# A hand-ordered five-engine pipeline: chosen rows sent through memory by index, decays by half the heads, and another order of steps

## The reference

```
x = x + gnn0(layernorm(x), adj)      # MLP, dense attention (512), MLP, masked attention: steps a_*, b_*
x = x + ffn0(layernorm(x))           # 127 chosen rows go through a GELU MLP: steps q_*
x = x + gat1(layernorm(x), adj)      # masked attention: steps g_*
x = x + mamba(layernorm(x))          # conv, silu, decays exp(segsum(dA)), gated norm, product: steps m_*

weights = x @ wr + br                # ffn0, x is layernormed
sel_idx = top_k(weights, 128)[:127]
y = gelu(x[sel_idx] @ w1 + b1) @ w2 + b2
out = zeros.at[sel_idx].set(y * weights[sel_idx]) + x
```

## Time and profile before

| | us |
|---|---|
| median of 3 runs | 3751.22 (3750.86 to 3752.01) |
| the profiled execution, its own time | 3752.41 |
| its span, first to last instruction | 3750.7 |
| PE busy | 3618.9 (96%) |
| PE weight loads busy, beside PE | 3158.1 (84%) |
| DVE busy | 2973.1 (79%) |
| ACT busy | 2364.2 (63%) |
| POOL busy | 993.9 (26%) |

### The profile page before, as it was taken

How to read it: one execution, slowest core, us unless ns; L and a number is a source line. 1 busy time by engine, 2 the same in 40 slices (tenths; PEclk the granted TensorE clock), 3 DMA queues, 4 the chain that set the end, 5 groups by cost and what they waited for, 6 DMA issues and landing times.

```text
span 3750.7 us, 63924 instructions
## 1 busy us (share of the span) xinstructions
PE 3618.9 (96%) x21016; PEld 3158.1 (84%) x21016; DVE 2973.1 (79%) x7729; ACT 2364.2 (63%) x5314; POOL 993.9 (26%) x1821
## 2 busy tenths in 40 slices
PE   6799999999999999999999999999999999999975
PEld 4688888888888888888888888888888888888864
DVE  3468878878888888888888888888887887888875
ACT  2356666667666666666666666666666666666654
POOL 0022232232232232232222223223223223223222
PEclk8899999999999999999999999999999999999998
DMA  3000100100100110110010010010010010010000
GB/s 102 12 26 32 39 28 31 39 28 31 39 28 31 39 36 23 39 39 23 36 39 28 31 39 28 31 39 28 31 39 28 31 39 28 31 39 29 30 29 31
DMA packets 73763, 126.85 MB, mean 34 GB/s; under 512 B 9984, under 2 KB 64128, under 8 KB 65536
## 3 DMA queue, kind: packets, MB, share of 16 engines
q1 hardware_dynamic: 69360, 126.39, 9.8%
q10 hardware_dynamic: 4368, 0.03, 0.1%
HBM read 109.10 MB, written 17.30 MB: 34 GB/s over the span
## 4 chain that ended last, share of the span: by engine, by line
PE 87%; DVE 8%; issue 2%; ACT 1%; POOL 0%; ACTq 0%; DVEq 0%; POOLq 0%
PE A L1199 12%; PE M L1335 7%; PE A L1219 7%; PE Q L1323 6%; PE A L1237 6%; PE A L1188 6%; PE Q L1316 6%; PE M L1369 6%; PE M L1428 6%; PE A L1284 3%; PE A L1246 3%; PE Q L1246 3%; PE Q L1284 3%; PE A L1229 2%; PE M L1357 2%
## 5 line engine op out<-in xcount | busy, mean ns | idle before, releaser
L1199 PE MATMUL A<-w_fc,o1T 128*128 128x256 f32 (+1 forms) x2048 | 454.7, 380 | 3.8 <-ACT o1T L541 3.8
L1199 PEld LDWEIGHTS A<-w_fc,o1T 128*128 128x128 f32 x2048 | 382.9, 189 | 57.8 <-ACT o1T L541 4.0
L433 POOL TENSOR_TENSOR var_m<-mv_m,epsilon 128x2 f32<-128x2 f32 x64 | 12.6, 197 | 1414.7 <-DVE mv_m L813 1414.7
L710 ACT ACTIVATE dec<-cumB,cumcol 128x256 f32<-128x256 f32 (+1 forms) x1024 | 366.2, 443 | 0.0
L1022 DVE SCALAR_TENSOR_TENSOR acc<-M,w_conv,acc 128x255 f32<-128x255 f32 (+2 forms) x768 | 315.0, 470 | 0.0
L1335 PE MATMUL M<-xT_m,w_in 128*128 128x256 f32 x1280 | 297.5, 379 | 0.8 <-DVE tz L1064 0.5
L1219 PE MATMUL A<-h,low 128*128 128x257 f32 (+1 forms) x1024 | 256.4, 395 | 22.9 <-DVE low L854 14.0
L1335 PEld LDWEIGHTS M<-xT_m,w_in 128*128 128x128 f32 x1280 | 237.7, 190 | 32.1 <-DVE tz L1064 2.0
L1323 PE MATMUL Q<-w_down,gsq 128*128 128x256 f32 x1024 | 241.2, 390 | 9.7 <-DVE gsq L995 9.7
L1316 PE MATMUL Q<-selT,w_up 128*128 128x128 f32 x2048 | 249.5, 275 | 0.9 <-ACT selT L646 0.9
L1064 DVE SCALAR_TENSOR_TENSOR tz<-tz,M 128x512 f32<-128x512 f32 x128 | 88.1, 688 | 202.5 <-ACT tz L693 202.5
(11 more groups left out here) (235 smaller groups left out, 8830.3 us busy)
## 6 DMA issues: line engine op xcount, KB each, us to landing
cumB<-cum_dram SPq DMA_DIRECT2D x64, 1024.0 KB, 4.7
x_in<-in_x SPq DMA_DIRECT2D x64, 256.0 KB, 2.8
x<-in_x SPq DMA_DIRECT2D x64, 256.0 KB, 2.9
out<-x3b SPq DMA_DIRECT2D x64, 256.0 KB, 2.8
w_mlp<-in_L_gnn_mlp_w SPq DMA_DIRECT2D x2, 512.0 KB, 6.3
w_fc<-in_L_gnn_W_fc SPq DMA_DIRECT2D x2, 512.0 KB, 8.6
w_up<-in_L_ffn_w SPq DMA_DIRECT2D x1, 1024.0 KB, 11.7
w_down<-in_L_ffn_w SPq DMA_DIRECT2D x1, 1024.0 KB, 12.9
```

The lines of the kernel that those rows point to most:

```text
L710: last = nc.scalar.activation(dec[:, h, :], columns[:, h, :], ACT.Relu, bias=cumcol[:, i, h:h + 1], scale=-1.0)
L1199: last = nc.tensor.matmul(rows1(half, u, 2), o1T[:, k, u * P:(u + 1) * P], w_fc[:, k, half, 0:D + 2 * i], start=(k == 0), stop=(k == KH - 1))
```

## The change

1. `q_gather` no longer forms the chosen rows by four products. DVE `q_rank` also writes `place`, the row number for each row: its rank, or rank + 1 from rank 127 on. A new POOL step `q_send` sends the two tiles of `xn_q` row by row to `sel_dram` with two indexed DMAs. A new SP step `q_sel` waits for both and loads the first 128 rows back to `sel`; PE `q_gather` waits for that and turns `sel` with two transposes. Row 127 is zeroed once, before the first turn.
2. The decays go by halves of the heads: four ACT steps and four DVE mixes instead of two; `m_y.0` waits for the first two mixes, `m_y.1` for all.
3. Long PE steps are two each (`q_ffn2`, `a_mlp2`, `m_z`, `m_out`), DVE's `m_silu` and POOL's `m_dt_log` too.
4. All five lists have another order and partly other lags.
5. DVE's `norm` waits for earlier readers in two cases (`a_xT_ps`, `sel_sent`); `m_scan` waits for the second `dec1` part of the graph before.

```diff
-    "tensor": [('q_gather', 3), ('b_att', 2), ('m_cum_col', 5), ('q_ffn1.0', 3), ('b_res', 2), ('q_ffn1.1', 3), ('a_mlp1.0', 1), ('a_mlp1.1', 1), ('m_xrow', 5), ('m_cb', 5), ('a_fc.0', 1), ('a_fc.1', 1), ('q_ffn2', 3), ('a_bcast', 1), ('m_turn', 4), ('q_scatter', 3), ('m_y.0', 5), ('m_y.1', 5), ('a_att.0', 1), ('g_turn', 3), ('a_att.1', 1), ('g_proj', 3), ('m_out', 5), ('g_bcast', 3), ('m_ss', 5), ('a_uturn', 1), ('m_dt', 4), ('q_route', 2), ('a_mlp2', 1), ('m_z', 4), ('g_pturn', 3), ('b_proj', 1), ('m_xbc_a', 4), ('b_bcast', 1), ('m_xbc_b', 4), ('m_da', 4), ('a_turn', 0), ('g_att', 3), ('b_pturn', 1)],
+    "tensor": [
+        ("m_da", 5), ("a_mlp1.0", 1), ("a_mlp1.1", 1), ("q_ffn1.1", 3), ("a_fc.0", 1), ("m_cum_col", 5),
+        ("a_fc.1", 1), ("m_cb", 5), ("a_bcast", 1), ("q_ffn2.0", 3), ("q_ffn2.1", 3), ("m_xrow", 5), ("q_scatter", 3),
+        ("a_att.0", 1), ("a_att.1", 1), ("m_y.0", 5), ("g_turn", 3), ("m_y.1", 5), ("g_proj", 3), ("m_turn", 4),
+        ("m_out.0", 5), ("g_bcast", 3), ("a_uturn", 1), ("m_out.1", 5), ("m_ss", 5), ("a_mlp2.0", 1), ("q_route", 2),
+        ("a_mlp2.1", 1), ("m_z.0", 4), ("b_proj", 1), ("m_dt", 4), ("g_pturn", 3), ("b_bcast", 1), ("m_z.1", 4),
+        ("g_att", 3), ("b_res", 1), ("b_pturn", 1), ("q_gather", 2), ("a_turn", 0), ("b_att", 1), ("m_xbc_a", 4),
+        ("m_xbc_b", 4), ("q_ffn1.0", 2),
+    ],
...
-    "scalar": [('a_att', 1), ('m_gated', 5), ('a_elu_b', 1), ('g_proj', 3), ('q_route', 2), ('m_dt_exp', 4), ('g_exp', 3), ('a_mlp2', 1), ('m_z', 4), ('b_proj', 1), ('g_pturn', 3), ('m_xbc_a', 4), ('m_xbc_b', 4), ('b_exp', 1), ('g_att', 3), ('b_pturn', 1), ('g_elu', 3), ('q_gather', 2), ('b_att', 1), ('b_elu_b', 1), ('a_turn', 0), ('m_silu', 4), ('q_gelu_a', 2), ('a_mlp1', 0), ('m_decay.0', 4), ('q_gelu_c', 2), ('m_decay.1', 4), ('m_xrow', 4), ('a_factors', 0), ('a_fcol', 0), ('g_turn', 2), ('m_turn', 3)],
+    "scalar": [
+        ("q_route", 2), ("a_mlp2", 1), ("g_exp", 3), ("b_proj", 1), ("m_dt_exp", 4), ("g_pturn", 3), ("m_z", 4),
+        ("b_exp", 1), ("g_elu", 3), ("b_pturn", 1), ("g_att", 3), ("q_gather", 2), ("b_att", 1), ("b_elu_b", 1),
+        ("m_xbc_a", 4), ("a_turn", 0), ("m_xbc_b", 4), ("a_mlp1", 0), ("q_gelu_a", 2), ("m_silu", 4), ("q_gelu_c", 2),
+        ("m_decay.0", 4), ("m_decay.1", 4), ("a_fcol", 0), ("a_factors", 0), ("m_xrow", 4), ("m_decay.2", 4),
+        ("m_decay.3", 4), ("a_att", 0), ("g_turn", 2), ("a_elu_b", 0), ("m_gated", 4), ("g_proj", 2), ("m_turn", 3),
+    ],
+    "gpsimd": [
+        ("q_norm", 3), ("m_xrow", 6), ("g_norm", 4), ("m_rms", 6), ("q_send", 3), ("m_dt_log.0", 5), ("m_turn", 5),
+        ("a_norm", 0), ("m_dt_log.1", 5), ("q_turn", 3), ("m_da", 5), ("m_norm", 4),
+    ],
+    "sync": [
+        ("m_store", 7), ("q_sel", 4), ("a_residual", 3), ("m_spread", 6), ("a_load", 0),
+    ],
...
+            def q_sel(b):
+
+                sp.wait_ge(sel_sent, 32 * b)
+                sp.dma_start(sel[:], sel_dram[0:P, :]).then_inc(sel_back, 16)
...
+                nc.gpsimd.dma_start(sel_dram[TOPK:TOPK + 1, :], tie_gap[0:1, 0, :]).then_inc(unused_row, 16)
+                pool.wait_ge(unused_row, 16)
...
+            def q_send(b):
+
+                after(S["place_ready"], b)
+                before(pool, S["sel_ps"], b)
+                pool.nop(nofuse=True)
+                for u in range(U):
+                    nc.gpsimd.indirect_dma_start(sel_dram, bass.IndirectOffsetOnAxis(place[:, u:u + 1], 0),
+                                                 xn["q"][:, u, :], None).then_inc(sel_sent, 16)
...
+                half, side = divmod(i, 2)
...
+                heads = slice(half * NH // 2, (half + 1) * NH // 2)
+                for h in range(heads.start, heads.stop):
+                    last = nc.scalar.activation(dec[:, h, :], columns[:, h, :], ACT.Relu, bias=cumcol[:, side, h:h + 1],
                                                 scale=-1.0)
...
+                nc.vector.scalar_tensor_tensor(out=place[:], in0=rank[:], scalar=float(TOPK), in1=rank[:], op0=ALU.is_ge,
+                                               op1=ALU.add).then_inc(S["place_ready"], 1)
...
+                pe.wait_ge(sel_back, 16 * b)
                 for c in range(KD):
-                    for u in range(U):
-                        last = nc.tensor.matmul(Q0[:, N + c * P:N + (c + 1) * P], xn["q"][:, u, c * P:(c + 1) * P],
-                                                pick[:, u, :], start=(u == 0), stop=(u == U - 1))
+                    last = nc.tensor.transpose(Q0[:, N + c * P:N + (c + 1) * P], sel[:, c * P:(c + 1) * P], ident[:])
...
-                pe.wait_ge(S["mix_ready"], nth(b, 2, 2))
+                pe.wait_ge(S["mix_ready"], nth(b, 4, 2 * i + 2))
```

More of the change, by code:

```diff
@@ new lines @@
+    "vector": [
+        ("a_elu_c", 2), ("q_norm", 3), ("m_sq", 6), ("a_uturn", 2), ("g_mask", 4), ("q_route", 3), ("g_lrelu", 4),
+        ("m_ms", 6), ("g_max", 4), ("q_rank", 3), ("b_proj", 2), ("m_out", 6), ("m_dt", 5), ("b_mask", 2),
+        ("g_pturn", 4), ("b_lrelu", 2), ("b_max", 2), ("a_stats", 0), ("m_gate", 5), ("g_elu_b", 4), ("b_pturn", 2),
+        ("g_x3", 4), ("a_norm", 0), ("m_stats", 4), ("b_elu_c", 2), ("b_x1", 2), ("m_conv_b.0", 5), ("m_scan", 5),
+        ("m_conv_b.1", 5), ("q_stats", 2), ("q_gelu_a", 3), ("m_conv_b.2", 5), ("q_gelu_b", 3), ("m_norm", 4),
+        ("m_cum_col", 5), ("m_silu_bc", 5), ("q_ffn2", 3), ("a_fc", 1), ("a_fcol", 1), ("m_silu", 5), ("a_maxima", 1),
+        ("m_cb", 5), ("m_mix.0", 5), ("q_scatter", 3), ("a_probs", 1), ("m_mix.1", 5), ("q_x2", 3), ("g_stats", 3),
+        ("a_att", 1), ("m_mix.2", 5), ("g_norm", 3), ("m_mix.3", 5), ("m_y.0", 5), ("m_y.1", 5), ("g_proj", 3),
+    ],
@@ L171, in gnn_ffn_mamba_kernel @@
         pick = sb("pick", [P, U, P])
+        place = sb("place", [P, U], U32)
+        sel = sb("sel", [P, D])
         pickT = sb("pickT", [P, N])
@@ L246, in gnn_ffn_mamba_kernel @@
         out_stored = sem("out_stored")
+        sel_sent = sem("sel_sent")
+        sel_back = sem("sel_back")
+        unused_row = sem("unused_row")
         DV, PL, PEs, AC = [sem(f"setup{i}") for i in range(4)]
@@ L371, in m_store @@
                 sp.dma_start(out[b - 1].rearrange("(u p) d -> p u d", p=P), x4[:]).then_inc(out_stored, 16)
-            turns(sp, "sync", dict(a_load=a_load, a_residual=a_residual, m_spread=m_spread, m_store=m_store), {})
+            turns(sp, "sync", dict(a_load=a_load, a_residual=a_residual, m_spread=m_spread, q_sel=q_sel, m_store=m_store), {})
             sp.wait_ge(cum_stored, 16 * B)
@@ L451, in _, with m_dt_log @@
             CHAIN = 13
-            def m_dt_log(b):
-                after(S["dt_e_ready"], b)
+            def m_dt_log(b, half):
+                if half == 0:
+                    after(S["dt_e_ready"], b)
                 w = dt_w
@@ L499, in _ @@
                 a_norm=rstd_of("a"), q_norm=rstd_of("q"), g_norm=rstd_of("g"), m_norm=rstd_of("m"),
-                q_turn=q_turn,
-                m_turn=m_turn, m_dt_log=m_dt_log, m_da=m_da, m_xrow=m_xrow,
+                q_turn=q_turn, q_send=q_send,
+                m_turn=m_turn, **parts("m_dt_log", m_dt_log, 2), m_da=m_da, m_xrow=m_xrow,
                 m_rms=m_rms), dict(a_norm=constants, m_turn=first_m_turn, m_da=first_m_da))
@@ L819, in step @@
                     v.wait_ge(S[f"{k}_rstd"], nth(b, 2, 2))
+                    if k == "a":
+                        before(v, S["a_xT_ps"], b)
+                    if k == "q" and not (isinstance(b, int) and b < 2):
+                        v.wait_ge(sel_sent, 32 * (b - 1))
                     for u in range(U):
```

114 lines of the change are left out of this document (63 added, 51 removed).

## The result

The changed kernel takes 3697.18 us (median of 4 runs, 3695.23 to 3697.78), the kernel before beside it 3751.61 (4 runs, 3750.86 to 3753.15): a ratio of 0.9853, 95% interval 0.9842 to 0.9865. Forecast were 3703 us (3690 to 3732) and faster with a chance of 0.87. The profiled execution took 3695.23 with a span of 3693.5, 57.2 us less than the span before.

What follows compares the result with a forecast made beforehand. PE's own work was taken to bound the full turns. From the old span of 3750.7 us, -41.3 (gather), -2 (thin turns' gather), +3 (thin edges) and -8 (end) gave 3702.4, as a median 3703, range 3690 to 3732.

Steps and rivals of the forecast that it cites:

- What bounds it: Full turns of 55.80 us: PE never waits, so only PE's own work or a new wait moves a turn.
- The gather, -0.70 a turn: PE `q_gather`: two transposes of 0.22 us replace 0.92 of products and `pick` transposes; -41.3 us over 59 full turns.
- The send's price, X = 1.4: POOL time per indexed send, taken as the middle between bounds of 0.30 and 2.42 us.
- The total of the path: PE `q_route` to `sel` landed: 7.85 + 2X = 10.65 us, under 11.36 of PE cover, spare 0.7.
- the two rivals of late rows: `sel` late at `q_gather`: partly, X 1.75 to 2.1, 3718 us, chance 0.14; wholly, slower, chance 0.10.
- Thin edges, +0.05 a turn: New order's barely covered PE waits, `b_bcast` and `b_att`: one short by 0.05 us, +3 in all.
- Thin turns at the end, -8: Last turns: -8 for `q_gelu_c` first, -6 for `xdt`, +4 for `q_gather`; -10 discounted to -8 us.
- Ahead, -2: Thin turns: the shorter gather counts partly, with two or three of five turns bound by PE; -2 us.
- The zeroed row, nothing, at most 3: POOL's first `a_norm` delayed by a DMA of some 2.8 us, while PE waited 5.13 for ACT; nothing, at most 3.
- Late rows, wholly: Rival at `q_gather`: wait of 0.82 us a turn eats the gains; 3781 us at the upper bound; chance 0.10.
- The thin edge: Rival in full turns: one barely covered PE wait short by 0.3 us a turn, +15, 3718 us; chance 0.08.
- The lock of POOL by DVE: DVE's `pick` could lock POOL's descriptor writing before the send, taking 0.48 of the 0.7 us spare; raises partly-late rival's chance.

Runs made afterwards that it cites:

- the two slowest kernels: Changed kernel with eight POOL additions ahead of the sends (5.5 us later), 3974.61 us; changed kernel with the decays whole, 3888.61 us.
- the kernel that differs in it alone: Changed kernel's lists and halves with the old four products, no `q_send` or `q_sel`: 3735.35 us, 0.9957 against the kernel before.
- the kernel with two additions: Changed kernel with two unused additions on POOL between `place` and the sends, 1.4 us later: 3699.81 us.
- The send with the zeroed row waited for later: Changed kernel with POOL's wait for the zeroed row moved from the start to ahead of the first `q_send`: 3692.31 us.
- the send in two places: Kernel before with the send added in its old order: `q_send` ahead of `m_dt_log`, 3829.29 us; behind `m_da`, 3759.15 us.
- send alone: Kernel before, old order and whole decays, with the indexed send replacing the products, `q_send` behind `m_da`: 3759.15 us.
- halves alone: Kernel before, old order and four products, with only decays and mixes by halves of the heads: 3769.02 us.

## Why the prediction was right, point by point

- **What bounds it: right.** Full turns nearly as long as PE's work, 55.80 before and 55.03 after. "In full turns PE never waits" was wrong by 0.15: the wait for `low` at `a_att` repeats in each of them. That only PE's own work and a new wait move a turn leaves out the clock, which adds to a wait in the two slowest kernels. Every kernel that was slower has a wait that repeats over 60 times.
- **The gather, -0.70 a turn: right.** 0.71 by the kernel that differs in it alone, with transposes of 0.22.
- **The send's price, X = 1.4 in bounds of 0.30 and 2.42: right**, 1.36 from start to start. The total of the path was too high, 10.65 said against 2312.2 - 2302.7 = 9.5 measured, by errors of both signs. The largest is in the sum itself: it adds X for the second send and then a landing on top, but a landing counts from the issue, so that X is in it already (in the kernel with two additions SP issues `sel` 2.45 after the second send's start, where the sum has X + 2.4 = 3.8). On the other side, the first send starts 3.08 us after `q_route` instead of 2.35: the rank is on time, but POOL begins 0.8 us after `place` is there. The landing of a half is 2.4 instead of 2.8 and that of `sel` 2.2. The path by itself would have ended earlier than the floor that `q_sel` behind `m_store` makes, 7.1 after `q_route` said and 7.34 measured. Spare was 0.7 said and 1.9 measured at PE, and the sends may come 0.5 later before that shrinks. So the two rivals of late rows, 0.24 together, were given too much: without the X counted twice the spare would have been 2.1. The Trainium skill (DMA: Bandwidth & Descriptors, "Anatomy of one DMA — SWDGE (gpsimd) path") gives by the prediction's estimate 2.3 us for a half and a spare of some 3. Its landing agrees with the 2.4 here; the spare doesn't, since SP's queue and the 0.8 at the start aren't in it.
- **Thin edges, +0.05 a turn: on the wrong side.** None was short; `b_att` starts 0.08 after the end of the copy `pT_b` (2314.79 against 2314.12 + 0.59). `m_dt` costs 0.81 in its new place instead of 0.88, and the wait of 0.15 for `low` is gone. Both together are more than the 0.06 a turn that the new lists give without the send, so other steps of PE take at least 0.1 more in them; which ones I haven't taken apart. Over 59 turns the sum said -41.3 + 3, measured -45.4.
- **Thin turns at the end, -8: measured -5.1, by another way.** The wait of `q_ffn2` went, as said, because `q_gelu_c` stands ahead of the decays; but the time was partly taken back by `m_cb` for `cT` and `m_da` for `dt`. The halves, put down for -3 in each of the last two turns, bring nothing alone, and in the changed kernel PE waits 4.10 + 4.15 for `xdt` in them instead of 0.97 + 7.16: what the last turn gains the one ahead of it loses. The send's cost there, +4 said, is 2.3.
- **Ahead, -2: measured -6.7.** The new lists bring 5.9 without the send; why so much in the first turns I haven't taken apart. The send with the zeroed row waited for later brings 238.3 - 234.6 = 3.7 more, where -2 was said, and the row takes 2.9 of that back.
- **The zeroed row, nothing, at most 3: mis-sized**, about 3 us. The step that failed is "some 2.8" for the DMA: beside the loads of the weights it took 6.4, so POOL came late enough to be PE's wait.
- **The rivals.** Late rows, wholly: didn't happen, but the mechanism is real, and its price "59 w" was too low: waits of 3.05 us made a full turn 59.37 - 55.03 = 4.3 longer in the mean, the rest by the clock that follows in 44 of 59 turns. The thin edge: didn't happen here, but it decides the old order (0.70 of 0.70 lost) and the place of `m_z` (1.09). The lock of POOL by DVE ahead of the send: the 0.8 us is no lock, for in the kernel with two additions POOL stands 0.79 at the same place with DVE idle.

The mechanism is right where most of the gain lies, in the full turns: 45.4 of 57.2 us against -38.3 said. In the thin turns, 11.8 against -10, the sum came out near by terms that missed in both directions, and that is luck.

What the forecast didn't see is why the order was needed. It asked whether the new order loses by thin edges; in the runs the old order kept nothing of the send's 0.70, with the send in two places and with `m_cum_col` moved, and the halves, a loss of 18 us in the old order, are worth 191 in the new. Other small changes of the old lists weren't tried, nor were the split steps one by one (`q_ffn2`, `a_mlp2`, `m_out`, `m_silu`, `m_dt_log`), nor the two changed waits on DVE. The three parts don't add: send alone +8, halves alone +18, order with halves -15, all together -54.

## What to carry to other kernels

Where one engine's own work is the turn, a shorter step gives its full length only if every copy and mix behind it has that much to spare; look for the step that stands next in the list and count from the last common start (here `q_route` to `b_att`, 17.90 with and without the products). An order in which the bound engine never waits holds only for the steps as they are cut: joining two halves on an engine that is idle a fifth of the time cost 5%, since others stand behind the long piece. A list of waits can leave out a short wait that repeats: compare a row's idle time with the waits that are counted for it. Put a slow step of a queue behind what is ready before it, and put a wait of the start where its result is first used.

## What the runs showed of the hardware

- An indexed send of 128 rows of 1 KB holds POOL for 1.01 us (0.96 to 1.10 over 128, in the kernel with two additions), 1.36 from start to start, and the first of a pair begins 0.79 us after POOL's own last instruction, in all 64 turns:

```profile
L501 POOL DMA_INDIRECT sel_dram<-xn_q,place x128: 962/1008/1102, 115.3 to 3571.7; - x128
```

- Small instructions of POOL take up to three times as long beside some of DVE's. The same multiplication of 16 columns, kernel before and kernel after (min, median, max in ns):

```profile
L462 POOL TENSOR_TENSOR dt_w<-log_c,dt_w x64: 222/223/224, 219.4 to 3711.7; 128x16 f32<-128x16 f32 x64
```

```profile
L514 POOL TENSOR_TENSOR dt_w<-log_c,dt_w x64: 221/652/657, 225.7 to 3659.4; 128x16 f32<-128x16 f32 x64
```

  In the full turn shown it runs from 2316.38 to 2317.03, beside DVE's sum of two SBUF tiles at 2316.26 to 2316.95. The other way round, `low` on DVE takes 2.20 us instead of 0.48 beside POOL's `xdt`. The Trainium skill (SBUF — State Buffer, "SBUF: two separate sides") describes such a lock between the two; these rows agree with it.
- A granted clock of 0.50 behind a wait of PE of 3.05 us, though PE was busy without a pause for the 44 us ahead of the wait, at 1.00. With such a wait in each turn the clock fell in 44 of 59 full turns; with waits of 0.61 and 1.30 in each, in 19 of 59; with one of 0.93, in none.
- A store of 1 KB to memory took 6.4 us at the start, while the weights were loaded (6.3 in the kernel that waits for it later).
